# Sum of squares, output product, root and output of a state-space stage moved from once per sequence to once per chunk

## The reference

```
x = x + Wo @ attention(groupnorm(x))                 # per picture, 1024 x 1024 scores
t = layernorm(tokens of x); xn = rmsnorm(t)          # state-space block, per sequence
z, xBC, dt = xn @ W_in.T                             # 256, 320 and 8 columns
xBC = silu(causal convolution of 4 taps over tokens)  # xs 8 heads x 32, B 32, C 32
state = state * exp(-dt*A) + (dt*xs) B^T;  y = state @ C + D*xs
y = y * silu(z);  y = y * rsqrt(mean(y*y) + 1e-5)     # mean over the 256 columns
t = x + t + y @ W_out.T
out = t + mixture of 8 experts, top 2 (layernorm(t))
```

## Time and profile before

| | before |
|---|---|
| median of 3 runs | 1116.74 us |
| the profiled execution | 1116.23 us, of which its span 1114.4 us |
| attention loop (about) | 0 to 320 us |
| scan loop, from its first `mixed` to the last gated chunk | 365 to 841 us |
| expert loop | 849 to 1114 us |
| PE, DVE, ACT, POOL busy over the span | 83, 64, 49, 21% |

### The profile page before, as it was taken

How to read it: one execution, slowest core, us unless ns; L and a number is a source line. 1 busy time by engine, 2 the same in 40 slices (tenths; PEclk the granted TensorE clock), 3 DMA queues, 4 the chain that set the end, 5 groups by cost and what they waited for, 6 DMA issues and landing times.

```text
span 1114.4 us, 20011 instructions
## 1 busy us (share of the span) xinstructions
PE 928.4 (83%) x7790; PEld 737.3 (66%) x7790; DVE 712.2 (64%) x1838; ACT 542.2 (49%) x859; POOL 236.8 (21%) x194
## 2 busy tenths in 40 slices
PE   3798899988986786878787797778979999999998
PEld 2554665556655575766676676667757878888877
DVE  2856776777662746364646446564566888878875
ACT  1534554444744653628273454626334455655453
POOL 0052001110104241414223141412532001111000
PEclk8899999999986778788878778787959999999999
DMA  5420000000002200203030200303010000000000
GB/s 148 153 114 19 19 20 2 19 20 20 1 9 57 49 19 15 52 2 65 1 67 1 47 20 8 60 1 66 7 53 1 20 1 20 20 20 20 20 1 39
DMA packets 30765, 36.16 MB, mean 32 GB/s; under 512 B 4560, under 2 KB 24784, under 8 KB 30672
## 3 DMA queue, kind: packets, MB, share of 16 engines
q1 hardware_dynamic: 29520, 30.68, 11.3%
q10 hardware_dynamic: 1152, 4.19, 1.0%
HBM read 21.50 MB, written 4.98 MB: 24 GB/s over the span
## 4 chain that ended last, share of the span: by engine, by line
PE 53%; DVE 28%; ACT 8%; issue 6%; POOL 2%; DMA 1%; SPq 1%; DVEq 0%; ACTq 0%; POOLq 0%
PE ps L1028 6%; DVE cacc L1682 6%; PE ps L684 5%; PE ps L947 4%; PE ps L763 3%; DVE acc L1959 3%; PE ps L765 3%; PE ps L764 3%; PE ps L671 3%; DVE nmax L1539 2%; PE ps L638 2%; ACT X L1234 2%; ACT un L1354 2%; PE ps L883 2%; PE ps L643 2%
## 5 line engine op out<-in xcount | busy, mean ns | idle before, releaser
L1773 DVE SCALAR_TENSOR_TENSOR dcy<-dcy,g_sb 128x1024 f32<-128x1024 f32 x64 | 95.4, 1491 | 117.9 <-ACT dcy L1310 117.5
L1959 DVE SCALAR_TENSOR_TENSOR acc<-ps,comb,acc 128x128 f32<-128x128 f32 x512 | 141.2, 344 | 21.5 <-PE ps L1028 20.6
L1028 PEld LDWEIGHTS ps<-w_f,hid 128*128 128x128 f32 x1024 | 131.2, 191 | 16.5 <-ACT hid L1373 8.2
L1028 PE MATMUL ps<-w_f,hid 128*128 128x128 f32 x1024 | 136.7, 277 | 4.8 <-ACT hid L1373 4.8
L1373 ACT ACTIVATE hid<-ps,b_f 128x512 f32<-128x512 f32 x128 | 86.3, 686 | 107.7 <-PE ps L765 107.4
L1310 ACT ACTIVATE dcy<-ps 128x1024 f32<-128x1024 f32 x64 | 65.4, 1021 | 134.9 <-PE ps L883 134.8
L1539 DVE TENSOR_REDUCE nmax<-ps 128x1 f32<-128x1024 f32 x64 | 78.1, 1221 | 39.7 <-PE ps L643 39.3
L518 POOL TENSOR_TENSOR xdt<-xs,dts 128x256 f32<-128x256 f32 x64 | 58.3, 913 | 211.6 <-PE ps L924 211.6
L1682 DVE SCALAR_TENSOR_TENSOR cacc<-ps,cw,cacc 128x1023 f32<-128x1023 f32 (+5 forms) x72 | 91.8, 1276 | 8.6 <-ACT cacc L1247 7.2
L1163 ACT ACTIVATE probs<-ps,nmax 128x1024 f32<-128x1024 f32 x64 | 71.3, 1114 | 41.3 <-DVE nmax L1539 38.4
L671 PEld LDWEIGHTS ps<-id_f,probs 128*128 128x128 f32 x512 | 60.0, 144 | 32.5 <-issue 22.9
(11 more groups left out here) (212 smaller groups left out, 1990.3 us busy)
## 6 DMA issues: line engine op xcount, KB each, us to landing
c_dec<-exp_dram SPq DMA_DIRECT2D x32, 256.0 KB, 5.1
xc<-in_x SPq DMA_DIRECT2D x8, 512.0 KB, 3.3
q_b<-q_a SPq DMA_DIRECT2D x16, 256.0 KB, 2.8
X<-in_x_tok ACTq DMA_DIRECT2D x8, 512.0 KB, 5.3
c_rep<-cacc SPq DMA_DIRECT2D x32, 128.0 KB, 2.4
out<-o_ch SPq DMA_DIRECT2D x8, 512.0 KB, 2.6
w_f<-in_w SPq DMA_DIRECT2D x2, 512.0 KB, 4.3
cst_f<-in_sel_rows SPq DMA_DIRECT2D x1, 512.0 KB, 5.8
```

The costliest lines, as they stand in the source:

```text
L1028: last = nc.tensor.matmul(ps[:, Y_BANKS[n], t * P:(t + 1) * P], hid[n % 2][:, t * P:(t + 1) * P], w2_f[:, e, :], start=True, stop=True)
L1773: nc.vector.scalar_tensor_tensor(mix[c % 2][:], dcy[c % 2][:], 1.0, g_sb[u][:, c:c + 1, :].to_broadcast([P, NH, P]), ALU.min, ALU.mult).th ...
L1959: done = nc.vector.scalar_tensor_tensor(acc[u][:, tt, :], ps[:, bank, t * P:(t + 1) * P], comb[u][:, tt, e:e + 1], acc[u][:, tt, :], ALU.m ...
```

## The change

`sum_of_squares`, `out_product`, `mean_square`, `root` and `output` now work on one chunk n = 8b + c. The product goes to the last 128 columns of bank 6 or 7, the bank that y of that chunk used, the mean square to column 256 of it. PE makes both for chunk n - 2 ahead of `output_rows` of chunk n; DVE makes the mean square of n - 2 behind the gated product of n, and `output` of n - 3 behind `mixed` of chunk c + 1. `hi_banks` are no longer used for it, so gates g = 1 waits only for the convolution of group 2, and comes first. Many entries of the tables stand earlier; `shortcut` (L1234) stands later. POOL's `decayed` and `weighted` are cut in two halves in different slots. The order of the silus of z is turned to match the gates.

```diff
-            def mean_square(b):
-                dve.wait_ge(m_squares_summed, b + 1)
...
+            def mean_square(n):
+                if n >= 4:
+                    dve.wait_ge(m_rms_ready, n - 3)
+                nc.vector.tensor_scalar(sve[:, n % 4:n % 4 + 1], ps[:, 6 + n % 2, DI:DI + 1], 1.0 / DI, GN2_EPS, ALU.mult,
+                                        ALU.add).then_inc(m_square_mean_ready, 1)
...
+            def output(n):
+                b, c = n // NT, n % NT
+                dve.wait_ge(m_rms_ready, n + 1)
+                if c == 0:
+                    dve.wait_ge(m_residual_ready, b + 1)
+                xb = X[:, b, c * P:(c + 1) * P]
+                nc.vector.scalar_tensor_tensor(xb, ps[:, 6 + n % 2, BANK - P:BANK], srs[:, n % 4:n % 4 + 1], xb,
+                                               ALU.mult, ALU.add).then_inc(m_out_added, 1)
@@ POOL
+            def root(n):
+                pool.wait_ge(m_square_mean_ready, n + 1)
+                nc.gpsimd.tensor_tensor(srs[:, n % 4:n % 4 + 1], sve[:, n % 4:n % 4 + 1], neg_half[:, 0:1],
+                                        ALU.pow).then_inc(m_rms_ready, 1)
...
+            pool_parts = [(totals, (), 3.5), (decayed, (0,), 3.5), (decayed, (1,), 4.5), (weighted, (0,), 5.5),
+                          (weighted, (1,), 6.5)]
...
                     if c + 1 < NT:
                         operand(b, u, c + 1)
-                    beside(b, u, first, last, c + 0.5)
+                    if n >= 2:
+                        root(n - 2)
+                    pieces(b, c + 0.5)
@@ PE
+            def out_product(n):
+                t = slice(n % NT * P, (n % NT + 1) * P)
+                for g in range(2):
+                    last = nc.tensor.matmul(ps[:, 6 + n % 2, BANK - P:BANK], y_t[:, g, t], w_out[:, g, :],
+                                            start=(g == 0), stop=(g == 1))
...
                     if c == 0:
                         decay(b, u, 0, first)
-                        if not first:
-                            pe.wait_ge(m_gated_ready, NT * b)
-                            sum_of_squares(b - 1, NT - 2)
-                            sum_of_squares(b - 1, NT - 1)
-                            out_product(b - 1)
                     pieces(b, c - 0.25)
                     if c + 1 < NT:
                         decay(b, u, c + 1)
                     pieces(b, c)
...
+                    if n >= 4:
+                        pe.wait_ge(m_out_added, n - 3)
+                    if n >= 2:
+                        pe.wait_ge(m_gated_ready, n - 1)
+                        sum_of_squares(n - 2)
+                        out_product(n - 2)
                     output_rows(b, u, c)
                     if c == 0:
+                        if n > 0:
+                            pe.wait_ge(m_gated_ready, n)
+                            pe.wait_ge(m_out_added, n - 2)
                         increments(b, u)
...
-            pe_parts = [(cumulate, (), 1, -0.25), (gates, (0, 0), 1, 0.5), (gates, (0, 1), 1, 0.5),
-                        (gates, (1, 0), 1, 1.5), (gates, (1, 1), 1, 1.5), (turn_x, (0,), 1, 2.5),
-                        (turn_x, (1,), 1, 2.5), (turn_b, (), 1, 3), (inner_products, (), 1, 3.5),
-                        (turn_normed, (), 2, 4), (steps, (), 2, 5), (group, (0, 0), 2, 5), (group, (0, 1), 2, 5),
-                        (group, (1, 0), 2, 5.5), (group, (1, 1), 2, 5.5), (group, (2, 0), 2, 6.75),
-                        (group, (2, 1), 2, 6.75)]
+            pe_parts = [(cumulate, (), 1, -0.25), (gates, (1, 0), 1, 0), (gates, (1, 1), 1, 0), (gates, (0, 0), 1, 0.5),
+                        (gates, (0, 1), 1, 0.5), (turn_x, (0,), 1, 2.5), (turn_x, (1,), 1, 2.5), (turn_b, (), 1, 3),
+                        (inner_products, (), 1, 3), (turn_normed, (), 2, 3.5), (steps, (), 2, 4.5),
+                        (group, (0, 0), 2, 4.5), (group, (0, 1), 2, 4.5), (group, (1, 0), 2, 5),
+                        (group, (1, 1), 2, 5), (group, (2, 0), 2, 6), (group, (2, 1), 2, 6)]
@@ ACT
-            act_parts = [(factors, (), 1, 0), (shortcut, (), 1, 0.5), (silus, (), 1, 1.5), (gather_x, (), 1, 2.75),
-                         (gather_b, (), 1, 3.5), (normed, (), 2, 3.5), (high, (), 2, 4.5), (steps, (), 2, 5.5),
-                         (tap, (0,), 2, 5.5), (softplus, (), 2, 6), (tap, (1,), 2, 6), (tap, (2,), 2, 7)]
+            act_parts = [(factors, (), 1, 0), (silus, (), 1, 1), (normed, (), 2, 2), (gather_x, (), 1, 2.75),
+                         (gather_b, (), 1, 3), (high, (), 2, 3.75), (shortcut, (), 1, 4), (steps, (), 2, 4.75),
+                         (tap, (0,), 2, 4.75), (tap, (1,), 2, 5.5), (softplus, (), 2, 5.5), (tap, (2,), 2, 6.5)]
@@ DVE
-            dve_parts = [("exponents", (), 1, -0.25), ("ends", (), 1, 1), ("inner", (), 1, 4), ("low", (), 2, 4.5),
-                         ("steps", (), 2, 5.5), ("conv", (0, 1), 2, 5.5), ("conv", (0, 2), 2, 5.75),
-                         ("conv", (0, 3), 2, 6), ("softplus", (0,), 2, 6), ("softplus", (1,), 2, 6),
-                         ("conv", (1, 1), 2, 6.5), ("conv", (1, 2), 2, 6.75), ("conv", (1, 3), 2, 7),
-                         ("conv", (2, 1), 2, 7.5), ("conv", (2, 2), 2, 7.5), ("conv", (2, 3), 2, 7.5)]
+            dve_parts = [("exponents", (), 1, -0.25), ("ends", (), 1, 1), ("inner", (), 1, 3.5), ("low", (), 2, 4),
+                         ("steps", (), 2, 5), ("conv", (0, 1), 2, 5), ("conv", (0, 2), 2, 5.5),
+                         ("conv", (0, 3), 2, 5.75), ("conv", (1, 1), 2, 6), ("softplus", (0,), 2, 6),
+                         ("softplus", (1,), 2, 6), ("conv", (1, 2), 2, 6.5), ("conv", (1, 3), 2, 6.75),
+                         ("conv", (2, 1), 2, 7), ("conv", (2, 2), 2, 7.5), ("conv", (2, 3), 2, 7.5)]
...
+                    n = NT * b + c
+                    if n >= 3:
+                        output(n - 3)
```

More of the change, by code:

```diff
@@ L531, in decayed, with weighted @@
                                           totals.to_broadcast([P, DS, NT - 2])).then_inc(m_decf_ready, 1)
+            def decayed(b, u, g):
                 pool.wait_ge(m_decf_ready, 2 * b + 2)
                 pool.wait_ge(m_c_spread, 64 * (b + 1))
[L534 to L539, removed]
+                rows = c_dec[u][:, 1:NT, g, :]
+                nc.gpsimd.tensor_tensor(rows, rows, c_rep[:, P:N].rearrange("p (c t) -> p c t", t=P),
+                                        ALU.mult).then_inc(m_c_decayed, 1)
+            def weighted(b, u, part):
                 pool.wait_ge(m_wend_ready, b + 1)
@@ L1120, in _ @@
             out_projection(B - 1)
-            for g in range(2):
+            for g in (1, 0):
                 for h in range(2):
@@ L1256, in silus @@
             def silus(b, u):
-                for g in range(2):
-                    act.wait_ge(m_z_product, 3 * b + 2 + g)
+                for g in (1, 0):
+                    act.wait_ge(m_z_product, 3 * b + 3 - g)
                     nc.scalar.activation(two(zs[u][:, g, :]), gate_banks(b, g), ACT.Silu).then_inc(m_z_ready, 1)
@@ L1818, in scan @@
                         mixed(b, u, 0)
-                        if not first:
-                            mean_square(b - 1)
                     if first:
@@ L1825, in scan @@
                         mixed(b, u, c + 1)
-                    if c == 1 and not first:
-                        output(b - 1, 1 - u)
+                    n = NT * b + c
+                    if n >= 3:
+                        output(n - 3)
                     if first:
@@ L1832, in scan @@
                     dve.wait_ge(m_z_ready, 2 * b + 2)
-                    if c == 0 and not first:
-                        dve.wait_ge(m_out_product, b)
                     r = slice(c * P, (c + 1) * P)
@@ L1837, in scan @@
                                             zs[u][:, :, r], ALU.mult).then_inc(m_gated_ready, 1)
+                    if n >= 2:
+                        mean_square(n - 2)
                     if c == 0:
@@ L2001, in _ @@
             scanned(dve, scan)
-            mean_square(B - 1)
-            output(B - 1, 1)
+            output(NT * B - 3)
+            for n in (NT * B - 2, NT * B - 1):
+                dve.wait_ge(m_tail_product, n - NT * B + 3)
+                mean_square(n)
+                output(n)
             scanned(dve, experts)
```

121 lines of the change are left out of this document (42 added, 79 removed).

## The result

The changed kernel takes 1137.22 us (median of 4 runs, 1136.14 to 1138.25), the one before 1116.72 (4 runs): ratio 1.018, 95% interval 1.015 to 1.021, so slower. The profiled execution took 1138.25 us, its span 1136.1. Forecast was 1123, with a range to 1138.

The account below looks back on a forecast made before the run. No engine is full; a loop of hand-offs bounds the scan, with half clock behind PE's waits. The profiled 1116.2 us + 11.5 (five periods of +2.3) - 4.7 (the end) = 1123 us; range 1099 to 1138.

Parts of the forecast that it names:

- The boundary: Start of a sequence: PE needs only the convolution's end for gates 1; y of chunk 1 at 9.5, gain 4.2 us.
- much slower rival: Both VectorE stalls in full (+2.4) and gates 1 at half clock: period up to 69.5, 1138 us; chance 0.14.
- the two stalls of VectorE: In the convolutions, VectorE waits for y of chunk 5 (0 to 1.6, taken 0.8) and chunk 6 (0 to 2.2, taken 0.6).
- Sequence 0 ... I count it as 0: Sequence 0 has neither an output nor that boundary, so no change in its time was counted.
- the end, -4.7: Sequence 7 to the first gelu: -3.8 + 3 for output products, -3.9 from last gated product to gelu; together -4.7 us.
- -3.8 + 3: Sequence 7 loses its `out_product` at the head (-3.8 us) but has eight inside, partly at half clock (+3).
- The upper edge, 1138: Top of the range, the much slower rival's time: period up to 69.5, +5.3 each, 26.5 - 4.7 in all.
- A new wait gives most of it back: Chunk 2: PE waits 6.5 us for the square behind `silus`, then half clock; y of chunk 2 at 21.0, gain left 3.2.
- +1.5 of added work: VectorE in the convolutions: a gated product, two outputs, three mean squares add 1.5 us, from 15.9 to 17.4.
- 3 to 5 us of slowed work: A PE wait costs itself plus some 3 to 5 us of half-clock work behind it, if on the path.
- the faster one (warm, 1101): Waiting for xl and group 2 costs no clock, VectorE never waits: period 62.2, 1101 us (1086 with quick restart); chance 0.30.
- that of no change: The period grows by no more than 1 us: 5 - 4.7 = 0, 1117 us; chance 0.14.

Follow-up runs that it names:

- e1: The changed kernel with silus back at slot 1.5, so that on ACT the square of chunk 0 stands ahead of it: 1139.0 us, ratio 1.022.
- e2: The changed kernel with gates 1 of sequence 1 behind y of chunk 1 again, inside sequence 0 alone: 1131.3 us, ratio 1.015.
- e4: The changed kernel's chunk-by-chunk outputs, but slots, order of gates and silus, and POOL's halves as in the kernel before: 1084.15 us, ratio 0.975.
- e7: e4 with the late slots of the changed kernel (steps and group 0 at 4.5, group 1 at 5, group 2 at 6): 1107.05 us, ratio 0.994.
- e5: The changed kernel with silus at slot 1.5 and ACT's normed at slot 3.5 again: 1123.68 us, ratio 1.008.
- e12: e4 with group 2 alone at slot 6, its tap at 6.5 and its first convolution at 7: 1120.87 us, ratio 1.002.
- e3: The changed kernel with 24 filler products on PE in chunk 2 of sequences 1 to 6, ahead of the sum of squares that waits: 1131.9 us, ratio 1.015.
- e9: e4 with filler products to unused bank columns in four places where PE waits, in sequences 1 to 6: 1086.81 us, ratio 0.972.
- e6: The changed kernel with normed alone at slot 3.5 again, silus still ahead of the square: 1135.86 us, ratio 1.020.
- e8: e4 with VectorE's steps and first convolution of group 0 at slot 5, ahead of the gated product of chunk 5: 1091.61 us, ratio 0.980.

## Why the prediction was right, and where it wasn't

*Right, in sequences 1 to 5.* The boundary: y of chunk 1 ends at t 10.9 (forecast 9.5); the rest comes with the half clock at gates g = 1, a condition that the prediction had in its much slower rival. In e1's sequences 2 to 4, where PE keeps the full clock there, it ends at 9.3. `silus` runs without a gap and ends at 16.8 (15.9). The new wait is 5.84 us (6.5), y of chunk 2 ends at 21.9 (21.0). `mixed` beside c_dec took 0.65 more than alone (1.1 was taken). xl ends at 37.5 (37.6), first convolution at 47.45 (47.7). The stretch is 17.55, against 17.4 + 1.4: of the two stalls of VectorE the one at y of chunk 5 didn't come, the other was 1.12 (0.6), and the work was 16.4 and not 17.4. The 15.9 that the prediction began with holds a stall of VectorE already, 0.68 us in this one sequence; the others of sequences 1 to 5 took 15.3. Clock over these periods 0.81 where I had "below 0.81". As forecast, no wait of VectorE on a root or of PE on an `output` shows in these sequences. The period is 65.0 (66.5); against the mean of before, 63.7, the five grew by 1.5 each, not by 2.3, which is the 4.2 us between +7.3 and +11.5.

*Wrong: "Sequence 0 ... I count it as 0".* It measured +13.3. The step was to argue from what sequence 0 lacks (no output, no boundary) instead of reading its order, which has every slot one later: gates g = 1 ahead of y there, 5.9 us by e2. It has the wait for the square too, 5.83 us, in full. Which slots make up the other 7.4 wasn't tried one by one; with the slots of before sequence 0 takes 64.1 (e4), with the late slots 66.2 (e7), and the changed kernel without the two early ones of ACT 73.5 (e5).

*Wrong: the end, -4.7.* It measured -1.6 from sequence 7 on, and +2.2 in sequence 6, which I didn't count and which has the wait for the square too. From the last gated product to the first gelu it took 6.1 us, not 3.9, before 7.8. The chain that I added up began with chunk 63's products right behind its square. They began at 867.34, as their bank waits for `output` of chunk 61, and that stood behind a sum of the experts. The first expert's products stand behind them on PE, and ACT loads its table only when those are there:

```profile
865.75 1.22 DVE L1930 TENSOR_TENSOR acc<-ps,acc 128x1024 f32<-128x1024 f32 x1 [0.84 <-PE ps L1056]
866.89 0.34 DVE L1789 SCALAR_TENSOR_TENSOR X<-ps,srs,X 128x128 f32<-128x128 f32 x1
867.34 0.58 PE L929 MATMUL ps<-ones_f,sqt 128*128 128x1 f32 x4 [0.80 <-issue]
869.25 1.28 ACT L1362 ACT_TABLE_LOAD   x1 [3.95 <-PE ps L766]
869.33 0.35 DVE L1789 SCALAR_TENSOR_TENSOR X<-ps,srs,X 128x128 f32<-128x128 f32 x1 [0.67 <-POOL srs L555]
```

From those products on the chain took what was forecast: the last `output` ended at 869.68, and the gelu began at 870.54, when the table was loaded. And the -3.8 + 3 up to the last gated product came as +0.1: from sequence 7's `mixed` it took 45.9 us, before 45.8. So the time of 1137 instead of 1123 is sequence 0 and the end; 18.6 us, less 4.2 of the periods.

*Luck.* That the kernel is slower was forecast for a part of its reason; that 1137 lies inside the range is luck. The upper edge, 1138, was the price of a cold boundary and two full stalls in every period; the periods grew by 1.5 and not by 5.3, and 13.3 us came from sequence 0, where no case of the prediction had anything. Nor does that edge follow from its terms: 66.5 with 2.4 and 3 more is 71.9, not 69.5, and no row says how much of it would be hidden.

*The reason given for the small gain was too narrow.* "A new wait gives most of it back" is true as an event, but taking it away alone gave nothing (e1): `normed` held the same path behind it. And the price that the forecast saw on VectorE (+1.5 of added work, part of 17.4) is smaller: e4 has two outputs and two mean squares in the stretch, no stall, and 15.94 against the 15.29 of before, 0.65 more. What is dear is the order: group 2 ahead of y of chunk 6, which the prediction had at 0.6 us, the smaller of its two stalls. In e12 it costs 4.6 directly. In the changed kernel, and in e7, PE's wait there is 2.5 to 2.7 us instead of 4.42; both have the first convolution ahead of the gated product of chunk 5, which e12 hasn't. That is the likely reason, though it wasn't tried alone.

*The clock.* In cold stretches y's last part took 1.08 us instead of 0.64, as the prediction had it. Its "3 to 5 us of slowed work" behind a wait is high: at 1.7 times the length, its own stretches of 5 and 9.8 us give 2.0 and 4.0, and those of the changed kernel, of 3.5 and 7, give 1.4 and 2.9. The Trainium skill ("HAM oscillation" of TensorE: Matmul & The Clock Gate) says that waits between bursts throw the clock back to half rate. The trace agrees for four of the five half-clock stretches of a period; at 666.7 us the clock fell with PE at work, and there the trace decides. And a wait doesn't settle it: behind waits of 2.18 and 0.46 us at the boundary the clock was at half in the changed kernel (639.5 to 643), and behind 2.17 and 0.46 in e1 it was full (PEclk 1.00 from 510.5 to 514 us). In e3, filling one wait moved the half-clock stretch to work in which no wait above 0.21 us stood. Of the rivals, the faster one (warm, 1101) and that of no change didn't come; of the much slower one the cold boundary came, without its price.

*Open.* Which early slot costs what: with two of them undone, e5 gave back 1.4 of their 3.5 us per period. What sets how long the clock stays at half. What a PE that is warm throughout would be worth, as the filler of e9 brought its own wait.

## What to carry to other kernels

A change that frees the path and a change that reorders around it should be timed apart: here the first was worth some -30 us (ratio 0.975) and the second some +50 on top (to 1.018), and the sum looked like a failure of the first. On an engine that works in order, an instruction moved earlier is free only if its input is there: each one moved ahead of its input holds what stands behind it, and while another wait lies beside it, taking it away alone shows nothing (e1, e5, e6). Where every slot is shifted for one iteration, that iteration has to be read by itself.

## What the runs showed of the hardware

One program can take two speeds in a steady loop, with the granted clock as the difference: periods of 57.5 and 62.0 us in turn (e8). With the same work behind the same wait of 1.41 us, the stretch at half clock lasted 3.4 or 3.5 us (e4, e8), 10.5 (e8) or 13.5 (e7).

`mixed` on VectorE, where it met c_dec on POOL, was held until POOL's instruction was over. It took 1.86 us in the changed kernel, 2.81 in the earlier trace rows and 1.47 in e4, against 1.21 alone:

```profile
671.50 2.09 POOL L536 TENSOR_TENSOR c_dec<-c_dec,c_rep 128x896 f32<-128x896 f32 x1
672.81 1.86 DVE L1762 SCALAR_TENSOR_TENSOR dcy<-dcy,g_sb 128x1024 f32<-128x1024 f32 x1 [1.83 <-ACT dcy L1299]
```

c_dec's half ends at 673.59 and `mixed` at 674.67, 1.08 later. So it is in every such meeting of all the traces, 1.08 or 1.09 us after the end of the half of c_dec during which `mixed` began, over durations from 1.21 to 3.17. The price is what is left of POOL's instruction when VectorE's starts, and so a matter of when they meet: 0.78 us here, 1.73 in the earlier trace rows, where the prediction could only take a middle.
